# Rows turned by a reload in quarters and VectorE, and separate PSUM banks for the down products, in the choice stage

## What is computed

```python
def _moe_forward(...):           # on xn; H = 1024, 32 experts, width 512
    logits = x @ router_w
    scores = sigmoid(logits)
    ...                          # choice of 8 of 32 experts, by groups
    routed = sum over the 8 chosen experts of silu(x @ w_gate) * (x @ w_up) @ w_down
    shared = silu(x @ sw_gate) * (x @ sw_up) @ sw_down     # width 1024
    return routed + shared

def _L0_attn_ref(...):           # on xn too
    x = layer_norm(feat_patch, ln_w, ln_b) @ in_proj_W.T   # 96 columns
    x = silu(conv of width 3 along the tokens)
    y = selective scan over the tokens
    return y @ out_proj_W.T + residual
```

## Time and profile before

| | us |
|---|---|
| median of 3 runs | 11737.64 |
| lowest and highest | 11735.35, 11744.92 |
| span of the profiled execution, first to last instruction | 11725.6 |
| TensorE busy in that span | 11315.7 (97%) |
| VectorE busy | 4553.4 (39%) |
| GpSimd busy | 4309.7 (37%) |
| ScalarE busy | 2971.0 (25%) |

### The profile page before, as it was taken

How to read it: one execution, slowest core, us unless ns; L and a number is a source line. 1 busy time by engine, 2 the same in 40 slices (tenths; PEclk the granted TensorE clock), 3 DMA queues, 4 the chain that set the end, 5 groups by cost and what they waited for, 6 DMA issues and landing times.

```text
span 11725.6 us, 206514 instructions
## 1 busy us (share of the span) xinstructions
PE 11315.7 (97%) x50496; PEld 9284.4 (79%) x50497; DVE 4553.4 (39%) x6239; ACT 2971.0 (25%) x4098; POOL 4309.7 (37%) x4236
## 2 busy tenths in 40 slices
PE   8999689998999999999999999999999999999998
PEld 7888567776888888888888878878887787888887
DVE  5666566664323323333323233232334324223222
ACT  2122144442222222222222222222223223222221
POOL 2555442221333333333333333333333333333333
PEclk9999889999999999999999999999999999999999
DMA  4333366765444444444544454454555545444443
GB/s 160 130 133 129 98 168 176 181 177 155 96 111 104 118 97 118 117 121 113 139 96 118 97 148 106 97 134 97 137 132 169 142 99 155 97 96 117 97 97 84
DMA packets 918207, 1451.50 MB, mean 124 GB/s; under 512 B 314530, under 2 KB 585058, under 8 KB 895048
## 3 DMA queue, kind: packets, MB, share of 16 engines
q0 software_dynamic: 212800, 623.06, 25.1%
q10 hardware_dynamic: 384512, 383.85, 11.7%
q1 hardware_dynamic: 320776, 443.28, 11.6%
HBM read 853.67 MB, written 596.15 MB: 124 GB/s over the span
## 4 chain that ended last, share of the span: by engine, by line
PE 66%; DVE 2%; DMA 2%; issue 2%; ACT 1%; DVEq 1%; ACTq 1%; POOL 0%; SPq 0%; POOLq 0%
PE pd L2009 22%; PE pg L66 7%; PE pg L68 7%; PE pg L67 7%; PE pu L68 7%; PE pu L66 7%; PE pu L67 7%; DVE w_lo L1911 2%; DMA activated<-av 2%; DVEq L1591 1%; ACT w_hi L1819 0%; DMA aq<-activated 0%; ACTq L1591 0%; ACT x_hi L1823 0%; DVE aT L1933 0%
## 5 line engine op out<-in xcount | busy, mean ns | idle before, releaser
L1782 POOL DMA_INDIRECT out_rows<-y,idx_s x528 | 863.4, 1635 | 4453.1 <-issue 4440.4
L1774 POOL DMA_INDIRECT xq<-xn_rows,idx_q x2124 | 2128.7, 1002 | 936.6 <-issue 486.8
L1823 ACT ACTIVATE x_hi<-xT 128x1024 fp32r<-128x1024 f32 x530 | 562.9, 1062 | 4564.8 <-DMA activated<-av 4389.2
L66 PE MATMUL pg<-w_hi,x_hi 128*128 128x512 f32 x4224 | 1646.3, 390 | 50.5 <-DVE x_lo L1926 39.8
L66 PE MATMUL pu<-w_hi,x_hi 128*128 128x512 f32 x4224 | 1645.1, 389 | 1.9 <-DVEq L1980 0.3
L67 PE MATMUL pg<-w_lo,x_hi 128*128 128x512 f32 x4224 | 1644.9, 389 | 0.0
L68 PE MATMUL pg<-w_hi,x_lo 128*128 128x512 f32 x4224 | 1644.8, 389 | 0.0
L67 PE MATMUL pu<-w_lo,x_hi 128*128 128x512 f32 x4224 | 1643.3, 389 | 0.0
L68 PE MATMUL pu<-w_hi,x_lo 128*128 128x512 f32 x4224 | 1643.3, 389 | 0.0
L1961 DVE SCALAR_TENSOR_TENSOR av<-pu,scale,sg 128x512 f32<-128x512 f32 x528 | 396.4, 751 | 3073.0 <-PE pu L68 2821.0
L1926 DVE TENSOR_TENSOR x_lo<-xT,x_hi 128x1024 fp32r<-128x1024 f32 x530 | 649.4, 1225 | 1555.8 <-ACT x_hi L1823 1552.3
(11 more groups left out here) (286 smaller groups left out, 14757.6 us busy)
## 6 DMA issues: line engine op xcount, KB each, us to landing
stage<-in_w_all SPq DMA_DIRECT2D x174, 1024.0 KB, 11.8
activated<-av ACTq DMA_DIRECT2D x528, 256.0 KB
aq<-activated ACTq DMA_DIRECT2D x528, 256.0 KB
rep<-steps ACTq DMA_DIRECT2D x192, 512.0 KB
xq<-xn_rows,idx_q POOLq DMA_INDIRECT x2124
xt<-in_x SPq DMA_DIRECT2D x64, 512.0 KB, 4.3
xn_rows<-xn SPq DMA_DIRECT2D x64, 512.0 KB, 2.6
xn_turned<-sx_hi SPq DMA_DIRECT2D x64, 512.0 KB
```

The costliest lines, as they stand in the source:

```text
L66: m(dst, hi, whi[:, cols], start=begin, stop=False)
L1774: g.indirect_dma_start(out=xq[q][:, n], out_offset=None, in_=xn_q, in_offset=bass.IndirectOffsetOnAxis(ap=idx_q[q][:, n:n + 1], axis=0))\
L1782: g.indirect_dma_start(out=out, out_offset=bass.IndirectOffsetOnAxis(ap=idx_s[q][:, 0:1], axis=0), in_=y[q][:], in_offset=None, compute_op ...
L1823: a.activation(x_hi[q][:].rearrange("p b (g j) -> p b g j", g=4), xT[:].rearrange("p (g b j) -> p b g j", g=4, b=KH), ACT.Copy).then_inc(x ...
```

## The change

It does four things in the choice stage.

1. The eight transposes of `turn_rows` on TensorE go away. Instead SyncE, having stored the xn of a tile to `xn_rows`, waits until that store has landed and loads it back in four transfers of 128 KB (`load_quarters`). Each reads, for 32 partitions, pieces of 256 numbers (1 KB). VectorE then turns the tile in one STREAM_TRANSPOSE of 128x1024, which turns blocks of 32x32 (`turn_rows` is now VectorE's), into `sxT`.
2. `x_high` becomes one copy of 128x1024 from SBUF, `x_low` one subtraction of 128x1024 with both inputs in SBUF, the copies into `xnT` are gone, and `project` reads `sxT`.
3. `down` writes two PSUM banks of its own (`spd0`, `spd1`), and waits for `y_ready` of the tile before instead of `sg_ready` and `av_ready`. The turned activated tile gets the bank `sta`. The gate and the up products now wait for `sg_ready` and `av_ready` of the tile before.
4. The hidden dimension comes out in another order, so the host lays out the shared, router and projection weights by quarters, as it did for the experts' already.

```diff
-        pd = (pg, pu)
-        tx = [pb(f"stx{i}", [P, 4, P]) for i in range(2)]
-        ta = tx[0]
+        pd = [pb(f"spd{i}", [P, 512]) for i in range(2)]
+        ta = pb("sta", [P, KI, P])
...
+            def load_quarters(c, k):
+                t = c * J + k
+                sp.wait_ge(xn_stored[k % 2], c * 32 + (k // 2 * 16 + 16))
+                if not (known(c, 0) and k == 0):
+                    sp.wait_ge(turned, t)
+                rows4 = rows(xn_d, t).rearrange("(g j) (a c) -> a j g c", g=4, a=4)
+                for a in range(4):
+                    sp.dma_start(xq[32 * a:32 * a + 32], rows4[a]).then_inc(xq_loaded, 16)
...
                     if not ends(c, k, 1):
                         store_turned(*later(c, k, 1))
+                    if not ends(c, k, 2):
+                        load_quarters(*later(c, k, 2))
                     if not (known(c, 0) and k == 0):
                         store_out(*later(c, k, -1))
...
             store_xn(0, 0)
+            load_quarters(0, 0)
             store_xn(0, 1)
+            load_quarters(0, 1)
...
             def x_high(c, k):
                 t = c * J + k
-                for h in range(2):
-                    act.wait_ge(tx_done, t * 2 + h + 1)
-                    if h == 0 and not (known(c, 0) and k < 2):
-                        act.wait_ge(xs_stored[k % 2], c * 64 + k // 2 * 32)
-                    a.activation(x_hi[k % 2][:, 4 * h:4 * h + 4], tx[h][:], ACT.Copy).then_inc(xh_ready, 1)
-                for h in range(2):
-                    if h == 0 and not (known(c, 0) and k == 0):
-                        act.wait_ge(lg_done, t)
-                    a.activation(xnT[:, 4 * h:4 * h + 4], tx[h][:], ACT.Copy).then_inc(xnT_ready, 1)
+                act.wait_ge(turned, t + 1)
+                if not (known(c, 0) and k < 2):
+                    act.wait_ge(xs_stored[k % 2], c * 64 + k // 2 * 32)
+                a.activation(x_hi[k % 2][:], xTv, ACT.Copy)\
+                    .then_inc(xh_ready, 1)
...
                 for h in range(2):
-                    if not ends(c, k, 0):
-                        pe.wait_ge((sg_ready, av_ready)[h], t + 1)
+                    if not (known(c, 0) and k == 1):
+                        pe.wait_ge(y_ready, t * 2 - 3 + h)
                     down_half(nc, pd[h][:], a_hi, a_lo, w_hi, w_lo, h).then_inc(down_done, 1)
...
-                    if not ends(c, k, 1):
-                        turn_rows(*later(c, k, 1))
...
+            def turn_rows(c, k):
+                t = c * J + k
+                dve.wait_ge(xq_loaded, t * 64 + 64)
+                if not (known(c, 0) and k == 0):
+                    dve.wait_ge(lg_done, t)
+                    dve.wait_ge(xl_ready, t)
+                v.transpose(xT[:].rearrange("p (b g j) -> p b g j", b=KH, g=4), xq[:].rearrange("p g (b i) -> p b g i", b=KH))\
+                    .then_inc(turned, 1)
...
                     if begun:
                         a_low(t - 1)
+                    if not ends(c, k, 1):
+                        turn_rows(*later(c, k, 1))
                     if not ends(c, k, 2):
                         norms(*later(c, k, 2), r if k < 2 else 1 - r)
                     activated(t)
```

More of the change, by code:

```diff
@@ L220, in route_stage @@
         out_stored = sems("out_stored", 4)
-        tx_done = sem("tx_done")
+        xq_loaded = sem("xq_loaded")
+        turned = sem("turned")
         xh_ready = sem("xh_ready")
-        xnT_ready = sem("xnT_ready")
         xl_ready = sem("xl_ready")
@@ L287, in store_turned @@
                 for n, (part, ready) in enumerate(((x_hi, xh_ready), (x_lo, xl_ready))):
-                    sp.wait_ge(ready, t * 2 + 2)
+                    sp.wait_ge(ready, t + 1)
                     sp.dma_start(xs_d[bass.ds(t * 2 + n, 1)].bitcast(F32).rearrange("a p h -> (a p) h"),
@@ L504, in _ @@
             pe.wait_ge(prep_done, 2)
[L506 to L515, removed]
-                        last = nc.tensor.transpose(tx[h][:, n], xn[k % 2][:, (4 * h + n) * P:(4 * h + n + 1) * P],
-                                                   ident[:])
-                    last.then_inc(tx_done, 1)
             def project(c, k, r):
-                pe.wait_ge(xnT_ready, (c * J + k) * 2 + 2)
+                pe.wait_ge(turned, c * J + k + 1)
                 if k == 0:
@@ L524, in project @@
                 for n in range(KH):
-                    last = nc.tensor.matmul(lg[r][:, k], xnT[:, n], wcat[:, n], start=n == 0, stop=n == KH - 1)
+                    last = nc.tensor.matmul(lg[r][:, k], xTv[:, n], wcat[:, n], start=n == 0, stop=n == KH - 1)
                 last.then_inc(lg_done, 1)
@@ L561, in chunk @@
                     begun = not (known(c, 0) and k == 0)
[L562 removed]
+                    pe.wait_ge(xl_ready, t + 1)
                     if not begun:
                         pe.wait_ge(split_lo, 2)
[L565 to L566 removed]
+                    else:
+                        pe.wait_ge(sg_ready, t)
                     gate_or_up(nc, pg[:], x_hi[k % 2], x_lo[k % 2], w_hi, w_lo, 0).then_inc(gate_done, 1)
@@ L585, in chunk @@
                     pe.wait_ge(av_ready, t + 1)
-                    if not ends(c, k, 1):
-                        pe.wait_ge(xnT_ready, t * 2 + 3)
-                        pe.wait_ge(xl_ready, t * 2 + 3)
                     for i in range(KI):
@@ L650, in weights_low @@
                 v.tensor_tensor(w_lo[q][:], stage[q % 2], w_hi[q][:], ALU.subtract).then_inc(split_lo, 1)
+            def turn_rows(c, k):
[6 more added lines that the diff above has]
+                    .then_inc(turned, 1)
             def x_low(c, k):
                 t = c * J + k
-                for h in range(2):
-                    dve.wait_ge(xh_ready, t * 2 + h + 1)
-                    if h == 0:
-                        dve.wait_ge(xnT_ready, t * 2 + 1)
-                        if not (known(c, 0) and k < 2):
-                            dve.wait_ge(xs_stored[k % 2], c * 64 + k // 2 * 32)
-                    else:
-                        dve.wait_ge(xnT_ready, t * 2 + 2)
-                    v.tensor_tensor(x_lo[k % 2][:, 4 * h:4 * h + 4], tx[h][:], x_hi[k % 2][:, 4 * h:4 * h + 4],
-                                    ALU.subtract).then_inc(xl_ready, 1)
+                dve.wait_ge(xh_ready, t + 1)
+                if not (known(c, 0) and k < 2):
+                    dve.wait_ge(xs_stored[k % 2], c * 64 + k // 2 * 32)
+                v.tensor_tensor(x_lo[k % 2][:], xTv, x_hi[k % 2][:], ALU.subtract)\
+                    .then_inc(xl_ready, 1)
             def a_low(t):
@@ L2065, in quarters @@
     def quarters(w):
-        return w.reshape(E, 4, KH, P // 4, I).transpose(0, 2, 1, 3, 4).reshape(E, H, I)
-    gate = np.concatenate([quarters(w_gate), halves(sw_gate)])
-    up = np.concatenate([quarters(w_up), halves(sw_up)])
+        return w.reshape(-1, 4, KH, P // 4, w.shape[-1]).transpose(0, 2, 1, 3, 4).reshape(-1, H, w.shape[-1])
+    gate = quarters(np.concatenate([w_gate, halves(sw_gate)]))
+    up = quarters(np.concatenate([w_up, halves(sw_up)]))
     def terms(w):
```

18 lines of the change are left out of this document (8 added, 10 removed).

## The result

The changed kernel's median is 11655.51 us of 5 runs (11642.48 to 11656.14), that of the kernel before 11740.97 of 5 (11735.35 to 11744.92). The ratio is 0.9923, interval 0.9912 to 0.9934: 0.77% faster, where 0.47% was forecast. So the sign was right and the forecast gain nearly two fifths too small.

What follows compares the result with a forecast made beforehand. TensorE's own stream plus its stops was taken to bound the choice stage. Terms -48.2 - 17.4 + 5 + 5 + 1 = -54.6 bring the span of 11725.6 to 11671.0; with 12.0 added, 11683 us, range 11655 to 11723.

Steps and rivals of the forecast that it cites:

- GpSimd's series: Scatters at k = 3 end 2 us later against the k = 0 gate: 5 us more, bounds 12 less to 26 more.
- The two main terms: Choice stage: transposes leaving TensorE, 48.2 us less, and down getting its own PSUM banks, 17.4 us less.
- Transposes off TensorE: TensorE's stream in the choice stage: 0.79 us a tile saved in 61 tiles, 48.2 us less.
- Own banks: Down's 21.4 us wait for `spu` goes, 4 us return waiting for `x_low`: 17.4 us less, bounds nothing or all back.
- Start: Choice stage's beginning: SyncE waits for xn's store and tile 0's turning, delaying weight loads; 5 us more, bounds 2.5 to 8.
- a rival for the whole stage: Choice stage: TensorE's stop moves to the next gate's wait for `x_low`, late from `a_high` or `base`; 11700 us, chance 0.15.
- End: Choice stage's last tiles: GpSimd starts its row of 24 scatters 1.2 later; 1 us more, bounds 10 less to 5 more.
- The ring of VectorE, GpSimd and ScalarE: Choice stage: these engines' cycle from series to series becomes the bound, 80.8 us a chunk; 11722 us, no change, chance 0.13.
- The late reload: Choice stage: the four reload pieces land one after the other, a tile takes 20.9 us; 11774 us, slower, chance 0.07.
- the 830 that I added up: VectorE's busy time in the choice stage's steady part, forecast to rise from 765 to 830 us in about 1150.
- the 10 that I had set as a sign of error: Scan or expert stage: a change by more than 10 us would show the prediction wrong.

Runs made afterwards that it cites:

- eight_back: The changed kernel with eight idle 128x128 transposes added on TensorE where the turning stood; median 11744.29 us, ratio 1.0010 to the kernel before.
- base_late: The kernel before with GpSimd's `base` moved behind the two powers, still ahead of the scatters; median 11714.78 us, ratio 0.9987.
- series_early: The changed kernel with GpSimd's eight scatters of a tile ahead of the second power instead of behind it; median 11660.40 us, ratio 0.9934.
- cut_both: The changed kernel with scatter series cut in three, two weight blocks loaded ahead of tile 1's reload, and the last two series paced; 11633.0 us, ratio 0.9912.
- turn_twice: The changed kernel with an idle 128x768 STREAM_TRANSPOSE ahead of each turning on VectorE; 11635.34 us, ratio 0.9914 to the kernel before.
- reload_late: The changed kernel with a tile's four reloads behind the store of the sum on SyncE's queue instead of ahead; 11641.47 us, ratio 0.9917.

## Why the forecast was too small

The choice stage gained 32.8 us more than the sum had. Of these 16.7 are the stops under GpSimd's series, a term with the wrong sign, 9.5 the own banks and 6.8 a cost of the transposes that the sum lacked. Against that, the up products took 0.9 more. The start was 4.8 worse than forecast and the end 5.4 better. The two main terms came as forecast in kind, and the 48.2 of the transposes alone made the sign safe.

**Transposes off TensorE.** 48.2 us, as summed. The step missed that the first product behind eight transposes costs more: down took 5.56 in tiles without a wait and takes 5.44 now. In 61 tiles that is 7 us, and eight_back gives 6.0 of them back. The trace of before showed it: 2.85 for the first half of down, 2.72 for the second.

**Own banks.** I gave back 4 of 21.4 us to the next wait, for `x_low`. The margin itself was nearly right: I put VectorE 0.4 ahead at k = 2, and in the changed kernel `x_low` ends there 0.04 us ahead at the least and 0.4 as the median; here in tile 30, 0.7 ahead of the next gate products at 638.32:

```profile
628.65 0.69 DVE L662 TENSOR_TENSOR sa_lo<-sta,sa_hi 128x512 fp32r<-128x512 f32 x1
629.25 1.23 DVE L649 STREAM_TRANSPOSE sxT<-sxq 128x1024 f32<-128x1024 f32 x1
...
636.42 1.22 DVE L657 TENSOR_TENSOR sx_lo<-sxT,sx_hi 128x1024 fp32r<-128x1024 f32 x1
```

But a thin margin costs nothing until it is used up; I charged 0.3 a tile for it. And the waits row names only what the record could pair: 21.4, where the sum of the down products gives 26.5 to 26.9. The term is -26.9, not -17.4. My cause of the wait was wrong besides: I put it down to parts 0 and 1 of `route`, and it was mostly (20 of 27 us, base_late) their collision with `base`, whose row I showed and used elsewhere.

**GpSimd's series.** The step that failed: "the series at k = 3 ends 2 us later against the gate of k = 0, where TensorE stopped", from which I took 5 us more. I read the stop by the series' end, because TensorE goes on 1.4 us behind it. But the later series left no stop instead of a longer one. Its beginning moved from 7.0 to 7.5 us ahead of the gate products of k = 0 to 2.5 to 4.6 ahead, and the stops were gone: -11.7 instead of +5. series_early moves it back and has them again. What holds TensorE during a series isn't shown by any run. The bound that I gave (12 less) held this case; I weighed it wrongly.

**Start.** +9.8 where I had +5 and bounds of 2.5 to 8. SyncE's queue:

```profile
28.43 0.43 SPq L284 DMA_DIRECT2D xn_rows<-xn  x1
34.02 1.74 SPq L295 DMA_DIRECT2D sxq<-xn_rows  x4
35.80 13.59 SPq L358 DMA_DIRECT2D bases<-in_w_all  x4
```

The loads begin 6.5 later than in the earlier trace rows, not 5, and the last low part of the weights is made at 58.04 instead of 50.00. Behind that, to the gate of tile 1, 1.7 more are lost. The turning of tile 1 (1.24) stands there now, and `x_low` of that tile, which has two SBUF inputs, met `base` and took 3.20 instead of 1.23; what gives the rest back stays open. This is the collision that I had as a rival for the whole stage and left out of the start:

```profile
69.29 3.20 DVE L657 TENSOR_TENSOR sx_lo<-sxT,sx_hi 128x1024 fp32r<-128x1024 f32 x1
```

**End.** -4.4, in the bounds of 10 less to 5 more. I held that GpSimd fixes this end. TensorE got through tile 62 without a stop and crawled in tile 63 instead, while ScalarE was held:

```profile
1258.54 0.60 ACT L470 ACTIVATE sa_hi<-sta 128x512 fp32r<-128x512 f32 x1 [24.54 <-remote]
```

cut_both shows that 8.5 us of it (88.3 to 79.7) go when the row of scatters is cut and spaced.

**The rivals.** The ring of VectorE, GpSimd and ScalarE isn't the bound: series follow each other by 17.5 us in three tiles of four, since `a_high` is late in fewer tiles than I took, and turn_twice, with 0.93 more in the ring, loses 0.1 us a tile. The late reload is out by reload_late; it lands some 4.7 us after its last issue (the median; 2.7 to 7.4), where I took 4.5. VectorE is busy 785 us of 1127, not the 830 that I added up, since collisions are fewer: the 56 operations that write z, for one, take 14.1 us in all instead of 38.2. Scan and expert stage moved by 13.3 and 3 us, the first above the 10 that I had set as a sign of error; the 14 executions show it to be scatter.

## What to carry to other kernels

Where an engine stops with no semaphore in sight, line up its stops with the other engines' long series in several tiles and compare the beginnings, not only the ends, and look too at the places where the same overlap stops nothing. A change that shifts their places by a few microseconds can be worth as much as the work that it removes. Before a wait is put down to a long stretch of work, look in that stretch for one operation that takes many times its own median. And a margin, however thin, isn't a cost: price it by what would use it up.

## What was new about the hardware

- Eight scatters in a row on GpSimd hold up engines that share nothing with them in the program. Cut into two, two and four, the same scatters take all 13 us of TensorE's stops away in 61 tiles. (The other 27 us of that run are the wait for `spu`, of which moving `base` alone takes 20.) ScalarE sat idle ahead of `a_high` 34 times from 300 to 1200, 332 us in all, with no semaphore that explains it, and with the cut never.
- Whether TensorE stops depends on where the series falls. At k = 0 there was no stop in 70 tiles where it began 5.2 us or less ahead of the gate products, and one of 0.2 to 2.9 us in 56 of 73 where it began earlier. At k = 1, 2 and 3 there was none at all, in 165 tiles with as early a beginning. What makes the difference is open, and five of the stops of before have no instruction packet near them.
- At the loop's turn TensorE lost 4.4 to 6.8 us at once (eight_back, five times).
- GpSimd's `base` of 2.40 us made an operation of 0.19 us on VectorE last 3.08. In each of twelve k = 2 tiles one operation met it so, and that alone was 20 us of TensorE's waiting.
- A stage that nobody touched took 1522.0 to 1535.4 us in 14 executions. Times of the whole kernel below that difference say little about one edit.
